# Three recurrent products computed as two halves of 64 columns, each half in a PSUM bank of its own

## What is computed

```python
x = x + rnn(x, cond)          # h = tanh(h @ Wh + x_t @ Wx + b), 2048 steps
x = x + attn(cond, x)         # a softmax over the 2 sequences, one weight per row
x = x + mlp(x, cond)          # tanh(x @ W_ih.T + cond @ W_hh.T + biases)
x = x + gru(x, cond)          # 2048 steps:
#   z = sigmoid([x_t, h] @ Wz + bz);  r = sigmoid([x_t, h] @ Wr + br)
#   c = tanh([x_t, r * h] @ Wh + bh); h_new = (1 - z) * h + z * c
#   every fourth step (but the last): h_next = tanh(h_new @ Wp + bp), else h_next = h_new
```

## Time and profile before

| | |
|---|---|
| median of 3 runs | 8802.99 us (8791.31 to 8805.06) |
| the profiled execution | 8793.52 us, its span 8791.7 us |
| TensorE busy | 8661.0 us, 99% of the span |
| TensorE weight loads | 6952.4 us, 79% |
| VectorE busy | 5044.1 us, 57% |
| ScalarE busy | 4687.6 us, 53% |
| GpSimd busy | 997.6 us, 11% |
| TensorE matmuls, weight loads | 291880 each |
| transfers of TensorE's code | 95, 1.56 MB |

### The profile page before, as it was taken

The page is one execution under the profiler, slowest core; times in us unless marked ns, Lnnn a source line. Parts: engine busy times, 40 slices in busy tenths (PEclk is TensorE's granted clock), DMA queues, the critical chain, the costliest instruction groups (busy, mean ns, idle before and its releaser), DMA issues.

```text
span 8791.7 us, 669547 instructions
## 1 busy us (share of the span) xinstructions
PE 8661.0 (99%) x291880; PEld 6952.4 (79%) x291880; DVE 5044.1 (57%) x26506; ACT 4687.6 (53%) x26367; POOL 997.6 (11%) x4362
## 2 busy tenths in 40 slices
PE   8999999999999999999999999999999999999998
PEld 6778777877787778778787778777877787778776
DVE  3555555555555555555555555555555555555555
ACT  3555555555555555555555555555555555555554
POOL 1111111111111111111111111111111111111110
PEclk8999999999999999999999999999999999999999
DMA  1000000000000000000000000000000000000000
GB/s 67 11 12 10 10 11 12 10 10 10 13 10 10 10 13 10 10 10 12 11 10 10 11 12 10 10 11 12 10 10 10 13 10 10 10 13 10 10 11 11
DMA packets 133369, 105.97 MB, mean 12 GB/s; under 512 B 14976, under 2 KB 132096, under 8 KB 132096
## 3 DMA queue, kind: packets, MB, share of 16 engines
q1 hardware_dynamic: 133248, 104.20, 3.9%
HBM read 62.20 MB, written 41.94 MB: 12 GB/s over the span
## 4 chain that ended last, share of the span: by engine, by line
PE 98%; issue 1%; DVE 0%; ACT 0%; DMA 0%; SPq 0%; POOL 0%; DVEq 0%; ACTq 0%
PE ps_r L398 23%; PE ps_c L398 22%; PE ps_l L398 21%; PE ps_z L398 20%; PE ps_p L398 6%; PE ps_mid L385 5%; PE ps_proj L385 2%; DVE l_T L536 0%; DVE ps_p L539 0%; PE ps_logit L434 0%; DMA rnn_h<-w_rnn_h 0%; DVE h_ring L647 0%; ACT l_ring L685 0%; ACT ps_l L659 0%; ACT scan_add L724 0%
## 5 line engine op out<-in xcount | busy, mean ns | idle before, releaser
L398 PE MATMUL ps_l<-rnn_h,l_ring 128*2 128x128 f32 x65536 | 2179.3, 274 | 26.8 <-ACT ps_l L659 26.8
L398 PE MATMUL ps_c<-c_h,rh 128*2 128x128 f32 x65536 | 2165.0, 272 | 6.3 <-DVE rh L602 2.4
L398 PEld LDWEIGHTS ps_c<-c_h,rh 128*2 128x2 f32 x65536 | 1397.2, 84 | 543.8 <-DVE rh L602 376.3
L398 PEld LDWEIGHTS ps_l<-rnn_h,l_ring 128*2 128x2 f32 x65536 | 1723.8, 85 | 112.2 <-ACT ps_l L659 36.9
L398 PE MATMUL ps_r<-r_h,h_ring 128*2 128x128 f32 x49152 | 1671.7, 272 | 18.7 <-DVE h_ring L647 18.7
L398 PE MATMUL ps_z<-z_h,h_ring 128*2 128x128 f32 x49152 | 1623.8, 273 | 0.2 <-issue 0.2
L398 PEld LDWEIGHTS ps_r<-r_h,h_ring 128*2 128x2 f32 x49152 | 994.9, 83 | 542.4 <-DVE h_ring L647 478.9
L398 PEld LDWEIGHTS ps_z<-z_h,h_ring 128*2 128x2 f32 x49152 | 1291.6, 85 | 50.4 <-issue 0.6
L539 DVE STREAM_TRANSPOSE ps_p<-ps_r 128x32 f32<-128x32 f32 x2048 | 473.4, 231 | 1329.0 <-PE ps_r L398 1329.0
L539 DVE STREAM_TRANSPOSE ps_p<-ps_c 128x32 f32<-128x32 f32 x2048 | 473.6, 231 | 1128.3 <-PE ps_c L398 1128.3
L319 POOL TENSOR_TENSOR y<-x,h_ring 128x8 f32<-128x8 f32 x2048 | 347.6, 201 | 4951.9 <-DVE h_ring L647 4951.9
(11 more groups left out here) (85 smaller groups left out, 9399.0 us busy)
## 6 DMA issues: line engine op xcount, KB each, us to landing
gates_spill<-gates_rows SPq DMA_DIRECT2D x128, 192.0 KB, 1.9
gates_seeds<-gates_spill SPq DMA_DIRECT2D x512, 48.0 KB
x_next<-xT SPq DMA_DIRECT2D x128, 64.0 KB, 1.7
x_mid<-xT SPq DMA_DIRECT2D x128, 64.0 KB, 1.7
rnn_spill<-rnn_rows SPq DMA_DIRECT2D x128, 64.0 KB, 1.5
rnn_seeds<-rnn_spill SPq DMA_DIRECT2D x512, 16.0 KB
y_out<-y SPq DMA_DIRECT2D x128, 64.0 KB, 1.6
rcz_x<-w_rc_x SPq DMA_DIRECT2D x1, 2048.0 KB, 9.0
```

Source lines behind the costliest of these rows:

```text
L398: last = nc.tensor.matmul(psum[QUAD * j:QUAD * j + B, 0:P], stationary(k), w[:, k, P * j:P * (j + 1)], start=False, stop=(k == KT - 1), sk ...
```

## The change

r, c and p are each computed as two halves of 64 columns of every block j. The low half (n = 0, tiles 0 and 1 of the result) goes to one bank, the high half (n = 1, tiles 2 and 3) to another: `ps_r` and `ps_c` become pairs of banks, and p shares the pair of c at other columns. The logits share the bank of `ps_proj`. A product of r, c or p is now 32 calls with 64 columns where it was 16 with 128; z, l and the rest are as they were. The order within a product is: k = 0 and 1 of the low half (*early*, they need only the low tiles of the state), then the rest of the low half, then the whole high half. Each half raises its own semaphore, and the transposes wait half by half. The pieces are of equal size (tiles 0, 1 and tiles 2, 3). At the fourth step of a group ScalarE seeds c only after p, since they share banks.

```diff
-FRONT = 1
+KH = KT // 2
+W = P // 2
...
-        ps_r, ps_z, ps_c, ps_l, ps_p, ps_logit, ps_mid, ps_proj = (
-            bank(n) for n in ("ps_r", "ps_z", "ps_c", "ps_l", "ps_p", "ps_logit", "ps_mid", "ps_proj"))
...
-        r_T, c_T, p_T = ([bank[:, P:2 * P].rearrange("p (k r) -> p k r", k=KT)[:, k, :] for bank, k in
-                          ((front, slice(0, FRONT)), (others, slice(FRONT, KT)))]
-                         for front, others in ((ps_p, ps_r), (ps_p, ps_c), (ps_r, ps_p)))
+        ps_z, ps_l, ps_mid, ps_proj = (bank(n) for n in ("ps_z", "ps_l", "ps_mid", "ps_proj"))
+        ps_r, ps_c = (ctx.enter_context(nc.psum_tensor(n, [P, 2, 512], fp32)) for n in ("ps_r", "ps_c"))
...
+        R_AT, C_AT, P_AT = 0, 0, W
+        r_T, c_T, p_T = ([pair[:, n, at:at + W].rearrange("p (k r) -> p k r", k=KH) for n in range(2)]
+                         for pair, at in ((ps_r, W), (ps_c, 2 * W), (ps_c, 3 * W)))
+        logits_at = slice(P, P + ROWS)
...
+            def halved_product(pair, at, stationary, w, ready, count, done, inc, early=((0, 0), (1, 0))):
...
+                def part(k, n):
+                    for j in range(NJ):
+                        last = nc.tensor.matmul(pair[QUAD * j:QUAD * j + B, n, at:at + W], stationary(k), w[:, k, P * j + W * n:P * j + W * (n + 1)],
+                                                start=False, stop=(k == KT - 1), skip_group_check=True)
+                    return last
+
+                if ready is not None:
+                    pe.wait_ge(ready[0], count)
+                for k, n in early:
+                    part(k, n)
+                if ready is not None:
+                    pe.wait_ge(ready[1], count)
+                for n in range(2):
+                    for k in range(KT):
+                        if (k, n) not in early:
+                            last = part(k, n)
+                    last.then_inc(done[n], inc)
...
-                        seeded_product(ps_r, state, r_h, ready, count).then_inc(r_product, 1)
+                        halved_product(ps_r, R_AT, state, r_h, ready, count, r_product, 1)
                         pe.wait_ge(z_seeded, t_gru + u + 1)
-                        seeded_product(ps_z, state, z_h, None, None).then_inc(z_product, 1)
-                        seeded_product(ps_c, lambda k: rh[:, k, :], c_h, rh_ready, t_gru + u + 1).then_inc(c_product, 1)
+                        seeded_product(ps_z, state, z_h).then_inc(z_product, 1)
+                        halved_product(ps_c, C_AT, lambda k: rh[:, k, :], c_h, rh_ready, t_gru + u + 1, c_product, 1)
...
-                            seeded_product(ps_p, lambda k: h_ring[:, u, k, :, 1], prop_w, h_ready, t_gru + PROP).then_inc(p_product, PROP)
+                            halved_product(ps_c, P_AT, lambda k: h_ring[:, u, k, :, 1], prop_w, h_ready, t_gru + PROP, p_product, PROP,
+                                           early=((0, 0), (1, 0)))
...
-            def transpose_piece(n, pieces, psum, T_done, inc=1):
-                nc.vector.transpose(pieces[n].rearrange("p k r -> p (k r)"), psum[:, PIECES[n][1]]).then_inc(T_done[n], inc)
-
-            def pieces_transposed(pieces, psum, T_done, inc=1):
-                for n in range(2):
-                    transpose_piece(n, pieces, psum, T_done, inc)
+            def transpose_piece(n, product, pair, at, pieces, T_done, count, inc=1):
+                dve.wait_ge(product[n], count)
+                nc.vector.transpose(pieces[n].rearrange("p k r -> p (k r)"), pair[:, n, at:at + W]).then_inc(T_done[n], inc)
...
-                        dve.wait_ge(r_product, t + 1)
-                        pieces_transposed(r_T, ps_r, r_T_done)
-                        for n, (k, _) in enumerate(PIECES):
+                        for n in range(2):
+                            transpose_piece(n, r_product, ps_r, R_AT, r_T, r_T_done, t + 1)
...
+            def seed_pair(pair, at, rows):
+                return nc.scalar.activation(pair[:, :, at:at + W], rows.rearrange("p (h n) -> p h n", h=2), ACT.Copy)
...
-                        seed_next_gate(i, u, 1, ps_c, c_T_done[1], c_seeded)
+                        if u % PROP < PROP - 1:
+                            seed_next_gate(i, u, 1, ps_c, c_T_done[1], c_seeded)
...
-                            seed(ps_p, bias_p[:, :]).then_inc(p_seeded, PROP)
+                            seed_pair(ps_c, P_AT, bias_p[:, :]).then_inc(p_seeded, PROP)
+
+                            seed_next_gate(i, u, 1, ps_c, c_T_done[1], c_seeded)
```

More of the change, by code:

```diff
@@ L63, in piece_sems @@
         def piece_sems(name):
-            return [sem(name + "_front"), sem(name + "_others")]
+            return [sem(name + "_low"), sem(name + "_high")]
         rnn_x = sb("rnn_x", KT, D)
@@ L214, in all_iterations @@
                 iteration(i)
-        PIECES = [(slice(0, FRONT), slice(0, QUAD * FRONT)), (slice(FRONT, KT), slice(QUAD * FRONT, P))]
+        PIECES = [slice(0, KH), slice(KH, KT)]
         block = ctx.enter_context(nc.Block())
@@ L387, in product, with seeded_product @@
                 return last
-            def seeded_product(psum, stationary, w, ready, count):
+            def seeded_product(psum, stationary, w):
                 for k in range(KT):
-                    if ready is not None and k in (0, FRONT):
-                        pe.wait_ge(ready[k // FRONT], count)
                     for j in range(NJ):
@@ L420, in _ @@
             pe.wait_ge(seeds_clear, 3)
-            for psum in (ps_l, ps_z, ps_p, ps_r, ps_c):
+            for psum in (ps_l, ps_z, ps_r[:, 0, :], ps_r[:, 1, :], ps_c[:, 0, :], ps_c[:, 1, :]):
                 open_bank(psum).then_inc(banks_open, 1)
@@ L433, in softmax_logits @@
                 for j in range(NJ):
-                    last = nc.tensor.matmul(ps_logit[QUAD * j:QUAD * (j + 1), 0:ROWS], ones[:, :], qx_sum[:, :], start=True, stop=True)
+                    last = nc.tensor.matmul(ps_proj[QUAD * j:QUAD * (j + 1), logits_at], ones[:, :], qx_sum[:, :], start=True, stop=True)
                 last.then_inc(logit_product, 1)
@@ L528, in _ @@
             tt = nc.vector.tensor_tensor
-            for psum in (ps_r, ps_z, ps_c, ps_l, ps_p, ps_logit, ps_mid, ps_proj):
+            for psum in (ps_r[:, 0, :], ps_r[:, 1, :], ps_z, ps_c[:, 0, :], ps_c[:, 1, :], ps_l, ps_mid, ps_proj):
                 last = nc.vector.memset(psum[:, :], 0.0)
@@ L591, in iteration @@
                     if gru:
-                        if u % PROP == 0:
-                            dve.wait_ge(p_seeded, t + PROP)
-                        dve.wait_ge(r_product, t + 1)
-                        pieces_transposed(r_T, ps_r, r_T_done)
-                        for n, (k, _) in enumerate(PIECES):
+                        for n in range(2):
+                            transpose_piece(n, r_product, ps_r, R_AT, r_T, r_T_done, t + 1)
+                        for n, k in enumerate(PIECES):
                             dve.wait_ge(r_tanh_done[n], t + 1)
@@ L631, in iteration @@
                     if gru:
-                        dve.wait_ge(c_product, t + 1)
-                        transpose_piece(0, c_T, ps_c, c_T_done)
+                        transpose_piece(0, c_product, ps_c, C_AT, c_T, c_T_done, t + 1)
                         dve.wait_ge(z_tanh_done, t + 1)
                         nc.vector.scalar_tensor_tensor(scan_add[:, :, :, 1], z_tanh[:, :, :], 1.0, h_neg_half[:, :, :], ALU.subtract, ALU.mult).then_inc(kept_done, 1)
-                        transpose_piece(1, c_T, ps_c, c_T_done)
-                        for n, (k, _) in enumerate(PIECES):
+                        transpose_piece(1, c_product, ps_c, C_AT, c_T, c_T_done, t + 1)
+                        for n, k in enumerate(PIECES):
                             dve.wait_ge(c_tanh_done[n], t + 1)
@@ L651, in iteration @@
                     if u % PROP == PROP - 1 and gru and not last_step(i, u):
-                        dve.wait_ge(p_product, t + 1)
-                        pieces_transposed(p_T, ps_p, p_T_done, PROP)
+                        for n in range(2):
+                            transpose_piece(n, p_product, ps_c, P_AT, p_T, p_T_done, t + 1, PROP)
             all_iterations(dve, iteration)
@@ L672, in seed_gate @@
                 after(act, T_done, STEPS * (i - LAG) + u)
-                seed(psum, gates_seeds[:, u, gate, :]).then_inc(seeded, 1)
+                if gate == 2:
+                    seed(psum, gates_seeds[:, u, gate, :]).then_inc(seeded, 1)
+                else:
+                    seed_pair(psum, R_AT if gate == 0 else C_AT, gates_seeds[:, u, gate, :]).then_inc(seeded, 1)
             def seed_next_gate(i, u, gate, psum, T_done, seeded):
```

16 lines of the change are left out of this document (8 added, 8 removed).

## The result

The change takes **16329.76 us** (median of 4 runs, 16322.92 to 16335.35) where the kernel before, beside it, takes 8799.64: a ratio of 1.856, 95% interval 1.853 to 1.859. The forecast was 8740 with a range to 9900. The profiled execution spans 16321.1 us.

A forecast was written before the change was run, and what follows sets the result against it. Bound by TensorE's pace plus 0.19 us of waits a step. Loop -355 + 71 + 108 = -176 us, written-out code +120: 8793.5 - 176 + 120 = 8738, said as 8740; own range 8605 to 8950, whole range to 9900.

The forecast's parts named there:

- rival 1: TensorE's loop code no longer stays on the core: 9830 us (27%) or 14.5 ms (8%), depending on what is refetched.
- the head alone: The ninth block pushes out only the loop's head, a stalled branch in each of 492 passes: +1085 us, 9830 us, 27%.
- the whole round: Every block of every loop pass is fetched again: 28.3 us a pass instead of 16.6, 14.5 ms, 8%.
- What it gains: In the loop, TensorE's waits before c, before r or p and inside r vanish: 2.9 us a chunk, -355 us.
- the halves' cost: Halved products of r, c and p take 0.016 us longer each, 36 a chunk: +0.6 us a chunk, +71 us.
- Rivals 2 and 3: First: waits stay or others replace them, 8940 to 9090 us, 9%; second: no gain left, 8785 to 8820 us, 8%.
- the slack of 0.13 us: Margin left in the loop's chain because the high half is awaited only behind c's early part, 0.22 us later.
- A halved product: On TensorE, 64 matmuls of 64 columns at 13.9 ns each: 0.887 us.
- The branches behind p: Shorter queued tail of p covers less of the branches: 0.22 us at four places a chunk, +0.9 us, +108 us.
- Rival 4: The branches cost nothing: 8605 to 8680 us, counted within the forecast's 48%.
- Code in the written-out iterations: Code fetch paces the last four iterations, 360 us instead of 271.7, and iteration 2, 100 instead of 68: +120 us.

The follow-up runs named there:

- the shortened change: The changed kernel with the loop's other work in fewer, wider calls over one contraction tile; run with heads apart (10464 us) and together (8770 us).
- change_one_block_less: The whole change with the outer loop's head, not the inner's, at a block's start, so both heads share a block: 15649 us, ratio 1.777.
- short_after: The changed kernel with the loop's other work in fewer, wider calls over one contraction tile, inner head at a block's start: 10464 us, ratio 1.190.
- halves_head_apart: Same work as halves_in_seven_blocks, but inner loop's head at a block's start and outer head in the block before: 9825 us, ratio 1.119.
- the padded kernels: The kernel before plus 95 or 143 matmul calls in the loop's code, run in one pass of 492 and otherwise branched past: 9507 and 9518 us.
- The shortened pair: Kernel before and change (heads sharing a block), both with other loop work in wider calls over one contraction tile: 8854 and 8770 us.
- short_after_one_block_less: short_after with one edit: the outer loop's head, not the inner's, at a block's start, so both heads share a block: 8770 us, ratio 0.996.
- halves_in_seven_blocks: The change, but p, c of the first step and all written-out iterations whole, both loop heads in one block: 8590 us, ratio 0.976.
- pad_8_blocks: The kernel before plus 143 matmul calls in the loop's last arm, run in one pass of 492 and otherwise branched past: 9518 us, ratio 1.082.

## Why the prediction was wrong

**The step that failed** is rival 1's chance and, in it, the count of blocks. "That ninth pushes out the loop's head" was right as a mechanism, and I gave it 35% in all, because "no limit shows in the trace". But the trace held no evidence for more than eight either, and I named the sequence "seven are known to be held. The change needs eight, and nine with the one that is fetched behind the end". Both ends of it are one block short, since the outer loop's head has a block of its own: eight were held before, and the change needs ten in a chunk, nine of them in every pass. The whole forecast of 8740 stood on room for more than eight, and the runs show that there is none: of the shortened change, nine blocks a chunk take 10464 us with up to 9 transfers, eight take 8770 with none.

**Which case of the rival.** I gave the head alone 27% (9830 us) and the whole round 8%. With a surplus in every pass (change, change_one_block_less) it is the round: each block is gone when the pass comes back for it. With a surplus only at the chunk's border it is the round once a chunk (short_after, halves_head_apart) or the single block (the padded kernels). A loss of the head alone in every pass, the case that I held likelier, showed in no run.

**The price of the whole round** was 28.3 us a pass, from 7 x 3.7 + 2.4. It took 32.1, nine blocks at 3.57: the pace was right, seven blocks should have been nine, and the block behind the end counts like the rest. 60.25 us a chunk over 123 chunks are 7411 us, with the 124 us below 7535; the profiled spans differ by 7529.

**The forecast's own terms held** where they could be seen:
- *What it gains, and the halves' cost.* Loop -176 us or -1.43 a chunk with the branches. The shortened pair with code held gives 68.4 - 66.6 = 1.8 us a chunk, less 0.2 to 0.27 for the heads (23 to 33 us over 123): 1.5 to 1.6. In full work, with seven of the nine products halved, 67.7 - 66.1 is 1.6. Rivals 2 and 3 are out: the slack of 0.13 us sufficed. In short_after_one_block_less, where all nine are halved and held, z to c and l to r are 0.87 us (z 4022.44, c 4023.31, l 4024.20, r 4025.08) in all steps but the third of the second pass, whose z to c is 1.03.
- *A halved product*: 0.89 us against 0.887, 0.893 in the mean of the loop.
- *The branches behind p*: 0.8 us a chunk against 0.9. Rival 4 is out. The agreement is partly luck: 0.22 was the middle between all and nothing for each place, and the four cost 0.37, 0.19, 0.19 and 0.06.
- *Code in the written-out iterations*: 362 - 271.7 and 102 - 68 are +124 us against +120.

**The Trainium skill** ("Runtime: NRT & Kernel Launch", Instruction fetch mechanics) gives TensorE's code store as a first-in, first-out one of 128 KiB, 2048 instructions in blocks of 256. That is eight blocks, which is what the runs show: 0 transfers with eight in a chunk, 9 in most chunks with nine. The chunks with 2 don't fit first in, first out. By it alone the prediction would have ended at the whole round. I cited it and then gave more weight to the silence of the trace. The same section has a taken branch to a block outside a window of two pages force a fetch; there the runs differ, since back edges out of the sixth block (before) and the seventh (halves_in_seven_blocks) cost no transfer.

**What stays open.** With nine blocks a chunk, the padded kernels lose two of them, short_after and halves_head_apart mostly nine and in some chunks two, with the same code. Giving up the oldest block explains the rounds of nine and not the twos; giving up the one that was longest unused would explain the twos and not the rounds. In pad_8_blocks the block that is jumped over isn't counted because no transfer for it shows; that it takes no room is a reading. The back edges stand at 156 and 92 instructions into their block in the padded kernels, at 239 and 223 in the other two; whether that tips it wasn't tried. And since all nine halved products of a pass don't fit in seven blocks, the change in full was never measured with its code held.

## What to carry to other kernels

Before lengthening the body of a loop, count its instructions in blocks, on the engine with the most: all blocks that the outermost cycle enters, the block of each loop's head, and one that is fetched ahead. Past eight the price here went from one stalled branch a chunk (5.6 us of 73.5) to every block of every pass (60 us of 128). If the trace shows a queue at rest and the body near a limit, treat the limit as unknown on both sides and don't let the silence of the trace speak for the case that you hope for; a stated size, where there is one, is then the best evidence.

Where a rewrite wins its waits but not its code, take the part that fits: the halves in seven of nine products, without those that shorten cover in front of a branch, and with both heads in one block, made the kernel 2.4% faster, 0.3 to 0.4% of it by the heads.

## What the runs showed of the hardware

- When all blocks are fetched, one comes every 3.8 us (the median in the change's loop; half of the gaps lie between 3.5 and 4.0), and TensorE needs less to run one here: a step of the change is 384 instructions (two halved products of 128, two whole ones of 64) in 3.53 us, so 2.35 us a block. The change's pass is bound by that: nine blocks, 32.1 us. Before, a step's 256 instructions took 3.67 us, which the fetch could just follow.
- A branch to a block that isn't held lasts 1.8 to 2.9 us past the other work and 2.7 to 5.2 us at the back edges and between the heads, by its single records in the change; the same branches in the kernel before last 0.07 to 0.21 us.
- The stalls lower the clock. Three windows of the change, ahead of the r at 4047.19, in the 3.2 us from it on, and behind:

```profile
4040.00:4047.00 7.00, 0.00 (x0) 0.00 (x0) 0.00 (x0) 0.00 (x0) 0.00 (x0) 0.50 0.09 23
4047.20:4050.40 3.20, 3.20 (x96) 2.80 (x100) 0.75 (x4) 0.52 (x3) 0.00 (x0) 0.52 0.02 5
4051.00:4056.00 5.00, 4.29 (x236) 3.94 (x228) 2.85 (x15) 2.42 (x15) 0.00 (x0) 1.00 0.08 20
```

  After 7 us without work the granted clock is at 0.50, the level of 1.2 GHz, and r and z then take 3.23 us instead of 1.76 (r at 4047.19 to c at 4050.42), 1.5 us more, before the clock is back at 2.4 GHz.
- Whether two loops' heads share a block costs nothing in work, and decided between 9825 and 8590 us for one and the same kernel.
